# A routed expert block whose 186 slots per expert are laid over the partitions as 128 + 58 instead of 96 + 90

## The chip, the cores and the metric

One NeuronCore of one Trainium2 chip runs the whole program in one launch. The metric is the device time in microseconds (us); the kernel before was run three times. An execution with the hardware profiler switched on is timed as well, and all instruction times below come from that execution.

## The reference

The input is 32 images of 3 x 96 x 96. They are cut into 36 patches each, projected to 256 features, given a class token and a position table (37 tokens per image, N = 32 x 37 = 1184 tokens), put through an attention-like block with running sums, and then through a mixture of 8 experts. The part that matters here is the last one:

```
logits = xf @ w_router + b_router            # 1184 x 8
topv, topi = top_k(softmax(logits), 2)       # two experts per token
cap = int(1.25 * n / e)                      # 185 slots per expert
pos = cumsum(onehot)[...] - 1 ; keep = pos < cap
buf[expert, slot] = xf[token]                # gather
h   = gelu(buf @ w1 + b1) ; out = h @ w2 + b2   # 185 x 256 -> 1024 -> 256
y[token] += weight * out[expert, slot]       # scatter, weights normalised per token
```

All data is float32 and the result is 1184 rows of 256 features.

## The kernel before

Capacity 185 is rounded up to `SL = 186` slots. TensorE multiplies matrices that have the feature dimension on the partitions and the 186 slots along the free dimension, so the up projection (`up`, line 1170), the first expert's down projection (`down`, line 1180) and the split-precision down projection (`down_split`, lines 1193 and 1195) always work on 186 or 2 x 186 columns. Slots lie over partitions only where rows of tokens are moved. There they need two tiles, because 186 is more than 128 partitions. Lines 16 to 21 set how:

```
SLOT_TILES = 2
SL = CAP + CAP % 2
ST = 96
SIZES = [min(ST, SL - s * ST) for s in range(SLOT_TILES)]   # [96, 90]
```

The places where `ST` and `SIZES` act, in the order of the work:

- VectorE, `find_slots` (line 938), builds `at_p`, a bf16 one-hot of `ST` columns for each of 11 token tiles and 2 choices. It is made in two pieces. The first covers token tiles 0 to 2 (2 x 3 x `ST` elements per partition) and runs ahead of `take_in(0, 0, first=True)` (line 890), which makes the first expert's input. The second covers tiles 3 to 10 (2 x 8 x `ST` elements), and `id_marks` (line 948) and `marks_ready` follow it.
- TensorE, `look_up` (line 995): 22 matmuls with a weight load of `at_p` (111 or 74 partitions by `ST` columns, bf16) each. It runs twice, once for the token numbers of the slots (32 moving columns) and once for the gate weights (48 moving columns). The result lies on `ST` partitions. VectorE turns the first result into `src_row` and `dst_row` (lines 866 to 871).
- GpSimd (POOL), `gather` (line 460), starts for each expert from 1 to 7 one indirect DMA per slot tile, which brings `SIZES[s]` rows of 1 KB each from `xrows` into `rows_in`. Expert 0 is not gathered; its input comes from matmuls with a one-hot matrix (`pick`).
- TensorE, `turn_in` (line 1158): four transposes per gathered expert, whose identity matrix, the moving operand, has `SIZES[s]` columns.
- TensorE, `turn_out` (line 1203): four transposes per expert, with weight loads of `SIZES[s]` columns and 128 moving columns.
- ScalarE, `weigh` (line 620), scales the rows in two instructions, of `SIZES[s]` partitions each.
- POOL, `add_out` (line 475), starts two indirect DMAs per expert, which add `SIZES[s]` rows of 1 KB to `out_rows`. Before the first of each expert it waits until both of the expert before have landed.
- The last expert goes another way: `down_rows` (lines 1216 to 1220) makes rows directly, with 24 matmuls per slot tile whose weight loads have `SIZES[s]` columns and which move 256 columns each. VectorE (line 984) scales a tile as soon as it is done, and each tile's scatter waits for that tile alone.
- Two plain DMAs on the SP queue have this shape as well: the zeros behind the output rows (line 389) and the last expert's bias rows (line 409).

The order of the work is written out by hand for each engine. From expert 1 to expert 6 a loop runs on every engine; on TensorE its body is `up` of pair 0, `turn_out` of the expert before, `up` of pairs 1 to 3, `down_split` with `turn_in` of the next expert in its middle. SP loads the next `w1` and `w2` (1 MB each) during the loop.

Of the kernel before, what the change touches and what calls it, by code (L numbers as in the profile page):

```python
# [16 lines left out]
SLOT_TILES = 2  # L17
PAIRS = KF // 2
SL = CAP + CAP % 2
ST = 96  # L20
SIZES = [min(ST, SL - s * ST) for s in range(SLOT_TILES)]
TB = 3
TT = TB * T
# [37 lines left out]
def constants():  # L61
# [13 lines left out]

    c[:, C_TRASH] = N + p + ST * (np.arange(SC)[None, :] % SLOT_TILES)
    c[:, C_EPS] = EPS
# [14 lines left out]
def vit_block(nc, first, patches, const, vectors, attn, w1, w2, b2_rows, xrows, out):  # L92
# [6 lines left out]
    with ExitStack() as ctx:  # L99
        def sb(name, shape, dt=f32):  # L100
            return ctx.enter_context(nc.sbuf_tensor(name, shape, dt))
# [9 lines left out]
        ids = cst[0:TT, C_IDS]  # L111
        trash = cst[0:ST, C_TRASH]
        eps_col = cst[:, C_EPS]
# [41 lines left out]
        onehot = sb("onehot", [TT, NT, SL])  # L155
        rows_in = [sb(f"rows_in{q}", [ST, SLOT_TILES, D]) for q in range(2)]
        def held(i, k):
            return first_t[:, :, :].rearrange("p k d -> p (k d)")[:, i * SL:(i + k) * SL].rearrange("p (k s) -> p k s", k=k)
# [3 lines left out]
        out_t, out_low = held(KF + 2 * KD, KD), held(KF + 3 * KD, KD)  # L162
        out_s = [sb(f"out_s{q}", [ST, SLOT_TILES, D]) for q in range(2)]

# [13 lines left out]
        neg_prefix = sb("neg_prefix", [TT, TT], bf16)  # L178
        zeros = sb("zeros", [ST, D])
        bn = sb("bn", [TT, 2 * NT, 6])  # L180
# [1119 lines left out]
```

How the kernel before makes its waits and increments, by code:

```python
        def drained(eng, kind, n):  # L310
            step = last_read(kind, n)
            if step in DVE_READS:
                eng.wait_ge(dve_drained, DVE_READS.index(step) + 1)
            else:
                eng.wait_ge(act_drained, ACT_READS.index(step) + 1)
# [14 lines left out]
        def filled(eng, kind, n):  # L331
            eng.wait_ge(psum_filled, PLACE[kind, n] + 1)
            return slots_at(n) if kind == "slots" else slot(kind, n)
# [26 lines left out]
        @block.sync  # L361
# [11 lines left out]
                    sp.dma_start(cst[:, :], const).then_inc(const_in, 16)  # L373
            def load_w1(e, q):
                sp.dma_start(w1_s[q], w1[e].rearrange("(k p) f -> p k f", p=128)).then_inc(w1_in[q], 16)
            def load_w2(e, q):
                sp.dma_start(w2_s[q], w2[e].rearrange("(k p) d -> p k d", p=128)).then_inc(w2_in[q], 16)
            for e in range(2):
                if e == 1:
                    sp.wait_ge(psum_filled, PLACE["proj", len(GROUPS) - 1] + 1)
                load_w1(e, e)
                load_w2(e, e)
            sp.wait_ge(pool_set, 2)
            for s, size in enumerate(SIZES):
                sp.dma_start(out[N + s * ST:N + s * ST + size], zeros[0:size, :]).then_inc(out_stored, 16)
# [13 lines left out]
                store_rows(out, h2, t0, n, out_stored)  # L404
            sp.wait_ge(gathered[1], 16 * SLOT_TILES)
            for n in range(len(GROUPS)):
# [3 lines left out]
                for q in range(2):  # L411
                    e = 2 * i + q + 2
                    sp.wait_ge(up_done, (e - 1) * PAIRS)
                    load_w1(e, q)
```

## Time and profile before

| | us |
|---|---|
| median of 3 runs (167.69 to 168.73) | 168.11 |
| profiled execution, its own time | 169.34 |
| span of that execution, first to last instruction | 167.5 |
| TensorE matmul busy | 157.5 (94%) |
| VectorE busy | 111.4 (67%) |
| ScalarE busy | 77.4 (46%) |
| POOL busy | 51.7 (31%) |

Busy times are unions of intervals; matmuls are pipelined, so their durations overlap and the distance between two starts is what one of them costs. "PEld" is the weight load of a matmul, on the same engine, "POOLq" and "PEq" are sequencers, "SPq" is the queue on which SyncE starts DMAs. L995 is line 995. The profiled execution's own time is 1.2 us above the median of the runs; the working below uses its durations as differences.

### The profile page before, as it was taken

Reading aid. Unit: us, or ns where it says so; the run is one execution under the profiler, and the core shown is the slowest. Engines: PE = TensorE matmul, PEld = TensorE weight load, DVE = VectorE, ACT = ScalarE, POOL = GpSimd, SP = SyncE. Lnnn points to the kernel's source line nnn. Section 1 sums busy time; section 2 is a strip of 40 time slices with the busy share of each in tenths; the row PEclk is TensorE's granted clock in tenths of the full one; section 3 lists DMA queues with packets and bytes.
Section 4 is the critical chain, followed back from the end, with each engine's and each line's share of the span. In section 5 each row is a group of like instructions: output and inputs, shape, how many; then the busy total and the mean of one; then the engine's idle time right before and its main releaser. Section 6 shows DMA issues by size and latency. Waiting matters only on the chain.

```text
span 167.5 us, 3069 instructions
## 1 busy us (share of the span) xinstructions
PE 157.5 (94%) x1041; PEld 148.2 (88%) x1041; DVE 111.4 (67%) x361; ACT 77.4 (46%) x186; POOL 51.7 (31%) x51
## 2 busy tenths in 40 slices
PE   7999999999999789989989999999999999999960
PEld 7679999986886689979989999999999999999950
DVE  0077673688588998396948876948669486694620
ACT  4306543526452309343705737657365583655300
POOL 2006213043021000000721735627266272703351
PEclk9999999999999955899999999999999999999995
DMA  5999930096014410620158789887888868820422
GB/s 164 429 411 420 386 125 0 9 337 206 0 29 134 122 45 4 195 59 4 45 175 308 144 287 268 248 266 137 287 253 255 263 145 276 245 22 6 46 25 22
DMA packets 17264, 28.48 MB, mean 170 GB/s; under 512 B 1289, under 2 KB 13875, under 8 KB 17125
## 3 DMA queue, kind: packets, MB, share of 16 engines
q1 hardware_dynamic: 14789, 25.48, 45.2%
q0 software_dynamic: 2464, 2.86, 10.0%
q8 instruction: 6, 0.10, 0.2%
q14 instruction: 5, 0.04, 0.1%
HBM read 24.20 MB, written 4.14 MB: 169 GB/s over the span
## 4 chain that ended last, share of the span: by engine, by line
PE 77%; DVE 14%; issue 2%; POOL 2%; DMA 1%; POOLq 1%; DVEq 0%
PE ps L1170 21%; PE ps L1193 11%; PE ps L1091 7%; PE ps L1076 6%; PE ps L1030 6%; PE ps L1195 5%; PE ps L1011 4%; DVE prod L777 2%; DVE z_s L775 2%; PE ps L1203 2%; PE ps L1042 2%; DVE onehot L752 2%; PE ps L1180 2%; PE ps L1158 2%; DMA rows_in<-xrows,src_row 1%
## 5 line engine op out<-in xcount | busy, mean ns | idle before, releaser
L475 POOL DMA_INDIRECT out_rows<-out_s,dst_row x16 | 23.7, 1483 | 40.4 <-ACT out_s L620 34.1
L596 ACT ACTIVATE first_t<-ps,b_cur 128x186 f32<-128x186 f32 x64 | 23.1, 412 | 25.5 <-PE ps L1170 25.5
L1193 PE MATMUL ps<-hid_hl,split 128*128 128x372 f32 x96 | 29.0, 369 | 0.0
L460 POOL DMA_INDIRECT rows_in<-xrows,src_row x14 | 15.7, 1124 | 33.2 <-DVE src_row L868 29.2
L1195 PE MATMUL ps<-hid_hl,split 128*128 128x186 f32 x96 | 23.9, 249 | 0.0
L1170 PE MATMUL ps<-first_t,w_even 128*128 128x186 f32 x128 | 21.8, 322 | 0.7 <-DVE first_t L890 0.7
L1170 PE MATMUL ps<-first_t,patch_t 128*128 128x186 f32 x128 | 21.6, 321 | 0.0
L899 DVE CAST hid_hl<-first_t 128x372 fp32r<-128x372 f32 x28 | 10.7, 383 | 16.1 <-ACT first_t L596 16.1
L1170 PEld LDWEIGHTS ps<-first_t,w_even 128*128 128x128 f32 x128 | 20.1, 190 | 1.0 <-issue 1.0
L1170 PEld LDWEIGHTS ps<-first_t,patch_t 128*128 128x128 f32 x128 | 20.1, 190 | 0.0
L1195 PEld LDWEIGHTS ps<-hid_hl,split 128*128 128x128 f32 x96 | 18.3, 191 | 0.0
L1193 PEld LDWEIGHTS ps<-hid_hl,split 128*128 128x128 f32 x96 | 18.0, 188 | 0.0
L498 ACT ACTIVATE split<-patch_t 128x512 fp32r<-128x512 f32 (+1 forms) x28 | 13.9, 559 | 7.8 <-DMA patch_t<-patches 5.0
L901 DVE TENSOR_TENSOR hid_hl<-first_t,hid_hl 128x372 fp32r<-128x372 f32 x28 | 15.3, 547 | 1.0
L514 ACT ACTIVATE xn<-ps,nmr,rstd 111x256 f32<-111x256 f32 (+1 forms) x22 | 10.7, 557 | 4.0 <-DVE nmr L682 4.0
L1076 PE MATMUL ps<-split 128*128 128x324 f32 x72 | 11.1, 312 | 0.0
L1076 PEld LDWEIGHTS ps<-split 128*128 128x128 f32 x72 | 10.7, 188 | 0.0
L661 DVE BATCH_NORM_STATS2 bn<-ps 111x6 f32<-111x256 f32 (+1 forms) x22 | 8.0, 417 | 3.8 <-PE ps L1106 2.7
L1011 PE MATMUL ps<-onehot,xn 111*128 111x186 f32 (+1 forms) x44 | 10.4, 409 | 0.1
L907 DVE TENSOR_TENSOR split<-patch_t,split 128x512 fp32r<-128x512 f32 x16 | 10.2, 685 | 0.0
L505 ACT ACTIVATE std<-mv,cst 111x3 f32<-111x3 f32 (+2 forms) x10 | 2.7, 294 | 16.0 <-DVE mv L664 16.0
L1011 PEld LDWEIGHTS ps<-onehot,xn 111*128 111x128 f32 (+1 forms) x44 | 9.8, 255 | 0.3 <-DVE by_expert L759 0.2
(165 smaller groups left out, 272.9 us busy)
## 6 DMA issues: line engine op xcount, KB each, us to landing
w_even<-w SPq DMA_DIRECT2D x8, 1024.0 KB, 5.3
patch_t<-w SPq DMA_DIRECT2D x8, 1024.0 KB, 5.3
patch_t<-patches SPq DMA_DIRECT2D x2, 972.0 KB, 11.2
att<-attn SPq DMA_DIRECT2D x1, 1280.0 KB, 8.4
first_t<-first SPq DMA_DIRECT2D x1, 870.0 KB, 6.0
xrows<-xn SPq DMA_DIRECT2D x3, 288.0 KB, 2.4
out_rows<-h SPq DMA_DIRECT2D x3, 288.0 KB
first_t<-first SPq DMA_DIRECT2D x1, 580.0 KB, 4.2
```

The source lines that it names most:

```text
L460: pool.indirect_dma_start(out=rows_in[q][0:SIZES[s], s, :], out_offset=None, in_=xrows[:, :], in_offset=bass.IndirectOffsetOnAxis(ap=src_r ...
L475: pool.indirect_dma_start(out=out[:, :], out_offset=bass.IndirectOffsetOnAxis(ap=dst_row[0:SIZES[s], c:c + 1], axis=0), in_=out_s[q][0:SIZ ...
L498: return act.activation(dst, src, ACT.Copy)
L514: ins = act.activation(xn[0:r, t], p[0:r, i * D:(i + 1) * D], ACT.Identity, bias=nmr[0:r, base + t:base + t + 1], scale=rstd[0:r, base + t ...
L596: ins = act.activation(hid[:, f, :], bank(pair)[:, (f % 2) * SL:(f % 2 + 1) * SL], ACT.Gelu, bias=b1_cur[q][:, f:f + 1])
L901: dve.tensor_tensor(hid_hl[:, f, 1], hid[:, f], hid_hl[:, f, 0], ALU.subtract).then_inc(hid_split, 1)
L1011: ins = pe.matmul(pick_slot[:, k, :], xn[0:r, t, k * 128:(k + 1) * 128], onehot[0:r, t, :], start=t == 0, stop=t == NT - 1)
L1076: ins = pe.matmul(p[:, d * 512:d * 512 + nb * NP2], w[:, k, d * 128:(d + 1) * 128], x[:, k, :], start=k + m == 0, stop=k == KP - 1 and m == 2)
L1091: ins = pe.matmul(p[:, d * 512:d * 512 + nb * NP2], tok_wt[:, k, d * 128:(d + 1) * 128], src[:, k, :], start=k == 0, stop=k == KP - 1)
L1170: ins = pe.matmul(bank(pair)[:, (f % 2) * SL:(f % 2 + 1) * SL], w1_s[q][:, k, f * 128:(f + 1) * 128], buf_t[q][:, k, :], start=k == 0, sto ...
L1193: pe.matmul(dst[:, 0:2 * SL], w2_h[q][:, f, cols], hid_hl[:, f].rearrange("p a s -> p (a s)"), start=f == 0, stop=False)
L1195: ins = pe.matmul(dst[:, 0:SL], w2_l[q][:, f, cols], hid_hl[:, f, 0], start=False, stop=f == KF - 1)
```

## The change

One constant. The slots of an expert stand as 128 + 58 over the partitions instead of 96 + 90; `SIZES` becomes `[128, 58]`.

```diff
 SLOT_TILES = 2
 PAIRS = KF // 2
 SL = CAP + CAP % 2
-ST = 96
+ST = 128
 SIZES = [min(ST, SL - s * ST) for s in range(SLOT_TILES)]
```

What it touches: `at_p` becomes 11 x 2 x 128 wide, `look_up` loads 128 weight columns, `slot_id`, `src_row`, `dst_row` and `coef` stand on 128 partitions, each gather and each scatter is 128 rows and 58 rows, the transposes are 128 and 58, and the two row products of the last expert make 128 and 58 rows.

## Rows read from the trace of the kernel before

**Rows 1.** The page, part 4: chain of work that ended last, by engine

```profile
PE 77%; DVE 14%; issue 2%; POOL 2%; DMA 1%; POOLq 1%; DVEq 0%
```

**Rows 2.** The same chain from 73 to 90 us: start, duration, what

```profile
77.49 1.18 PE ps L995 x22
...
80.19 1.15 POOL rows_in L460
...
81.64 2.36 DMA rows_in<-xrows,src_row
```

**Rows 3.** Waits from 73 to 90 us: who waited for whom, us, times, longest

```profile
PEld ps L1158 <- DMA rows_in<-xrows,src_row: 0.8, 1, 0.8
PE ps L1170 <- DVE first_t L890: 0.7, 1, 0.7
PEld ps L995 <- DVE id_marks L948: 0.4, 1, 0.4
```

**Rows 4.** Groups by line and form: shapes, count, busy us, mean ns, idle before

```profile
L938 DVE TENSOR_TENSOR at_p<-cst,slot_p 111x1536 bf16<-111x1536 f32 x1 | 1.8, 1752 | 0.0
L938 DVE TENSOR_TENSOR at_p<-cst,slot_p 111x576 bf16<-111x576 f32 x1 | 0.8, 750 | 0.0
L995 PE MATMUL ps<-w_marks,at_p 111*96 111x48 bf16 x20 | 1.0, 202 | 0.0
L995 PEld LDWEIGHTS ps<-w_marks,at_p 111*96 111x96 bf16 x20 | 1.0, 125 | 0.0
L1146 PEld LDWEIGHTS ps<-chosen,ones 111*111 111x111 bf16 x5 | 0.3, 133 | 0.0
L1158 PE MATMUL ps<-cst,rows_in 90*128 90x90 f32 x14 | 2.9, 242 | 0.0
L1203 PE MATMUL ps<-cst,first_t 128*90 128x128 f32 x14 | 2.7, 273 | 0.0
```

**Rows 5.** Timeline of TensorE around bf16 loads: start, first start to last end

```profile
69.38 0.34 PEld L1146 LDWEIGHTS ps<-chosen,ones 111*111 111x111 bf16 x5
77.49 1.06 PEld L995 LDWEIGHTS ps<-id_marks,at_p 111*96 111x96 bf16 x22 [0.37 <-DVE id_marks L948]
84.69 0.23 PE L995 MATMUL ps<-w_marks,at_p 111*96 111x48 bf16 x2
```

**Rows 6.** Timeline of TensorE in the expert loop: both kinds of transposes

```profile
95.43 0.49 PE L1158 MATMUL ps<-cst,rows_in 96*128 96x96 f32 x4
99.89 0.60 PE L1203 MATMUL ps<-cst,first_t 128*96 128x128 f32 x4
```

**Rows 7.** Timeline of TensorE and POOL in the last expert

```profile
158.67 0.28 PE L1220 MATMUL ps<-split,hid_hl 128*96 128x256 f32 x1
160.00 1.45 POOL L475 DMA_INDIRECT out_rows<-out_s,dst_row  x1 [3.10 <-DVE out_s L984]
161.49 0.28 PE L1220 MATMUL ps<-split,hid_hl 128*90 128x256 f32 x1
162.59 1.47 POOL L475 DMA_INDIRECT out_rows<-out_s,dst_row  x1 [1.14 <-DVE out_s L984]
```

**Rows 8.** DMA, 83.2 to 84.2 us, the 90-row gather: queue, packets, MB, share

```profile
q0 software_dynamic: 48, 0.09, 31.6%
```

**Rows 9.** DMA of the 96-row scatter (161.9 to 163.2), then the 90-row (164.5 to 167.5)

```profile
DMA packets 112, 0.10 MB, mean 76 GB/s; under 512 B 16, under 2 KB 112, under 8 KB 112
...
DMA packets 112, 0.09 MB, mean 31 GB/s; under 512 B 22, under 2 KB 112, under 8 KB 112
q0 software_dynamic: 112, 0.09, 30.9%
```

**Rows 10.** Windows: stretch, length, busy of PE, PEld, DVE, ACT, POOL, PEclk, DMA

```profile
56.00:58.00 2.00, 1.43 (x14) 1.43 (x15) 1.86 (x16) 0.00 (x0) 0.00 (x0) 1.00 0.63 169
58.00:60.00 2.00, 1.65 (x14) 1.59 (x13) 1.93 (x14) 0.00 (x0) 0.00 (x0) 0.50 0.57 172
74.00:76.00 2.00, 1.36 (x9) 1.39 (x10) 2.00 (x5) 0.27 (x2) 0.00 (x0) 1.00 0.00 0
```

## The prediction

> **What bounds the kernel now.** I read the chain of waits first. It lies on TensorE for 77% of the span, on VectorE for 14% and on GpSimd and DMA for a few per cent [rows 1]. So TensorE sets the time, except in short stretches, and an edit is worth what it does to TensorE's spacing or to one of those stretches. The change touches three places of the second half: the set-up of the slots (73 to 90 us), the loop over experts, and the last expert's tail. The part of the chain from 73 to 90 us shows that the set-up is serial: behind at_p and the marks on VectorE come the look-up on TensorE, the first gather's start on POOL and the landing of its second DMA [rows 2]. The waits of that stretch say where TensorE stood still: 0.7 us for the first expert's input, which VectorE makes behind the first piece of at_p, 0.4 us for the marks behind the second piece, 0.8 us for the first gather [rows 3]. Afterwards the chain stays on TensorE to its last product: the list of waits has no later one of it on a gather or a scatter. The end is one VectorE instruction, one scatter and its landing [rows 7].
>
> **at_p gets wider.** The two pieces of 576 and 1536 elements took 750 and 1752 ns [rows 4]. The slope is 1002/960 = 1.044 ns per element. They become 768 and 2048 elements: +192 is +0.20 us, +512 is +0.53 us. The first delays take_in(0) and with it TensorE, which was waiting for just that [rows 3]; the second delays the marks, for which TensorE also waits, and nothing else covers it. Both lie on the path: +0.73 us.
>
> **Look-ups, 2 x 22 matmuls.** The weight load grows from 96 to 128 bf16 columns. From the timeline, the 22 loads take 1.06 us from first start to last end with 0.125 us for one, so (1.06 - 0.125)/21 = 44.5 ns apart; the 5 loads of 111 columns are (0.34 - 0.133)/4 = 52 ns apart [rows 4, 5]. The moving side has 32 and 48 columns, and with a load ready in time two such matmuls stood (0.23 - 0.202) = 28 ns apart [rows 4, 5]. So the load sets the spacing and costs 0.5 ns per column: 128 columns give 60.5 ns, +16 ns x 44 = +0.70 us. Bounds: 28 ns apart (44 x -16.5 = -0.73 us) if the load stops limiting, and 83 ns, the distance at which 128-column f32 loads are known to fit (transposes, below), +1.7 us. I take +0.70, since the two nearest widths lie on that line. The first look-up delays src_row and the gather, the second delays TensorE itself; both are on the path.
>
> Against this stands a rule. The Trainium skill, page "TensorE: Matmul & The Clock Gate", section "Weight-path perf modes — Fast Weight Load (FWL) and DoubleRow", says that loads of exactly 128 non-fp32 weight columns take a faster path by themselves. No bf16 load of 128 columns is in this trace. By the rule the 44 loads would get cheaper rather than dearer; that is rival 1.
>
> **Gathers.** POOL's issue time does not follow the rows: the last 96-row scatter took 1.45 us and the 90-row one 1.47, and that is kept [rows 7]. Only the first gather is on the path, and there its second DMA, since that is issued 1.45 us after the first and lands last [rows 2]. That DMA kept the 16 engines 31.6% busy over 1 us, 5.06 engine-us; over 15 engines with data that is 0.34 us for 6 rows each [rows 8]. With 58 rows over 16 engines it is 4 rows each: -0.10 us (bounds 0 and -0.2). The 128-row DMA before it gets 8 rows per engine instead of 6, ends some 0.1 us later, and has over a microsecond until the second's data. The later gathers are issued a whole expert ahead, and TensorE waits for none of them; uncovered, each would move by the same 0.1 us.
>
> **Transposes.** turn_in: four starts within 0.49 us, (0.49 - 0.242)/3 = 83 ns apart at 96 and 90 moving columns, with a load of 128 columns for each. turn_out: (0.60 - 0.273)/3 = 109 ns apart at 128 moving columns [rows 4, 6]. So a 128-column move costs 109 ns; one of 58 lies between 58/128 x 109 = 49 ns (move-bound) and 83 ns (bound by its 128-column load, which is known to fit in 83). Per expert 2 x 109 + 2 x (49 to 83) against 332 ns: -16 to +52 ns; I take 61 ns for the short one, the spacing a 128-column load gets above, +8 ns. Seven experts: +0.06, rounded to +0.1 us (-0.1 to +0.4). turn_out keeps its 128 moving columns at 109 ns, which hides a load of 128 (83) as well as 96: 0, or up to 16 ns for each expert's first load, which I leave in the range.
>
> **Last expert.** The row products with 90-column loads stand (161.49 - 158.67)/24 = 117.5 ns apart [rows 7]. The 256 moving columns set that. 128 and 58 change nothing: a 128-column load fits in 83 ns. ScalarE's and VectorE's instructions keep their free sizes; the partitions of a tile do not appear in their durations (the groups of L984 and L620 at 96 and 90 partitions agree).
>
> **Tail.** The last scatter's DMA kept 16 engines 30.9% busy over 3 us: 14.8 engine-us over 96 slots of 6 on each engine, 0.155 us a row, 0.93 us an engine [rows 9]. 58 rows are 4 per engine: -0.31 us (bounds 0 and -0.4), right at the end of the span. The 128-row scatter ahead of it gets 0.31 us longer but its data move from 162 us on and the last one's only after 164.5 [rows 9].
>
> **The plain DMAs.** The zeros are stored in the first half and asked for by the first scatter; the bias rows (128 KB for 96) are loaded ahead of the loop and used in the last expert. The loop and the set-up hide them; uncovered, 32 KB more at the gather's rate (0.34 us for 90 KB) is 0.1 us.
>
> **Sum.** 0.73 + 0.70 - 0.10 + 0.10 - 0.31 = +1.12 us. On the profiled execution that is 169.34 + 1.12 = 170.5; that execution stands 1.23 us above the median of the runs, 168.11, to which I apply the same difference: 169.2 us, +0.7%. A measurement of this kernel tells no less than 1% (1.7 us) from no change, so this is "no change", on the slow side.
>
> **Rival 1: the wide loads are quick.** If a 128-column bf16 load no longer limits, the moving side does: 28 ns apart, 44 x -16.5 = -0.73 us. Sum 0.73 - 0.73 - 0.10 + 0.10 - 0.31 = -0.31 us, 167.8 us. For it: these 44 are the only loads that change from another width to 128 in bf16. Against: the line through 96 and 111 columns. This is the case of the skill's rule named above.
>
> **Rival 2, slower: 58 rows go over two engines.** If a DMA's rows are dealt only to as many engines as divide their number, 96 goes to 16, 90 to 15, 128 to 16, but 58 = 2 x 29 to two, 29 rows each. It decides from the size at which the divisor falls below the engines needed to stay hidden, here at two places. The first gather: 29/6 x 0.34 = 1.64 us instead of 0.34, +1.30 us. The last scatter: 29 x 0.155 = 4.5 us instead of 0.93, +3.6 us. In between POOL's idle time before scatters hides it. Total 0.73 + 0.70 + 0.10 + 1.30 + 3.6 = +6.4 us, 174.5 us (about 172.5 if accumulating rows pipeline better in a long run). What speaks against it: the 96-row scatter left 112 packets of which 16 are small, that is 96 rows and one semaphore write per engine; the 90-row one also left 112, of which 22 small, so 90 rows were filled up to 96 with 6 tiny packets [rows 9]. Filling up to a multiple of 16 is dealing by 16, and 58 would be filled to 64. It is not conclusive, since 15 x 6 rows and one engine of 6 fillers is also what divisor dealing with equal rings leaves.
>
> The Trainium skill, page "DMA: Bandwidth & Descriptors", section "Why a DMA increments its semaphore by 16 and not by 1", states the divisor rule, and also an exception measured on software-generated direct copies, rounded up over 16 engines. The packet counts here sit with the exception.
>
> **Rival 3: the clock falls.** TensorE's granted clock went to 0.50 (1.2 GHz) at 58 us after 2 us with 1.43 us busy in thin products; in 74 to 76 us with 1.36 us busy it stayed at 1.00 (2.4 GHz) [rows 10]. The change adds 0.2 and 0.53 us of standing and thinner look-ups there. A fall like the one at 58 us, over about 10 us of work, costs up to 5 us: 174. Against it: dense products lie between the gaps.
>
> **How the numbers follow.** Main case 0.53 (169.2; its own bounds 168.2 to 170.2), rival 1 0.27 (167.8), rival 2 0.09, rival 3 0.04, something unforeseen 0.07 on both sides. The predicted time is the main case's. The range 167.4 to 170.4 takes in the main case with its bounds and rival 1 with some noise of the runs (0.5 us each way), and leaves out rivals 2 and 3 and most of the unforeseen, 0.18. Slower by over 1% means above 169.8: rivals 2 and 3, a fifth of the main case (0.11), half the unforeseen: 0.27. Faster means below 166.4: 0.04. Within 1%: 0.69.
>
> **What would show it.** at_p at 0.95 and 2.29 us; TensorE's waits before the first expert and before the look-up longer by 0.2 and 0.5 us; the 22 look-up loads 60 ns apart (right) or about 30 (rival 1); in the last scatter 80 packets, 64 + 16, with 22 under 512 B, and its landing about 0.3 us sooner after issue (right), or a landing 3 us and more later with a low DMA share (rival 2); turn_in's four transposes in about 0.50 us; the clock at 1.00 from 68 us to the last product (else rival 3). Wrong would be a new wait of TensorE inside the loop, or a look-up or DMA whose cost does not follow these rows.

## The result and the profile after

The changed kernel takes 183.33 us (median of 4 runs, 182.31 to 184.81) against 168.38 us for the kernel before on the same chip. The ratio is 1.089, 95% interval 1.084 to 1.094: 15 us slower. Forecast was 169.2 us (167.4 to 170.4). The profiled execution has a span of 181.5 us, 14.0 more than before. Here and below the ratios leave out the few executions of the chip's slower state (the longest were one of 864.71 us of the version with 80 moved rows and one of 260.51 us of the kernel before).

The page of the changed kernel: span, DMA packets, the software queue, and the chain that ended last.

```profile
span 181.5 us, 3069 instructions
...
DMA packets 21155, 28.55 MB, mean 157 GB/s; under 512 B 5246, under 2 KB 17878, under 8 KB 21016
...
q0 software_dynamic: 6336, 2.90, 10.7%
...
PE 49%; DMA 20%; DVE 14%; POOL 5%; issue 4%; ACT 2%; POOLq 1%; ACTq 0%; DVEq 0%
DMA out_rows<-out_s,dst_row 18%; PE ps L1170 7%; PE ps L1091 6%; PE ps L1076 6%; PE ps L1030 6%; PE ps L1193 5%; POOL out_rows L475 4%; PE ps L1011 4%; DMA rows_in<-xrows,src_row 2%; PE ps L1180 2%; PE ps L1195 2%; PE ps L1158 2%; ACT out_s L620 2%; DVE prod L777 2%; DVE z_s L775 2%
```

Before, 77% of the chain lay on TensorE and the DMAs had 1% [rows 1]. Now the scatters alone hold 18%. The software queue, which carries the indirect DMAs, moves nearly the same bytes (2.90 MB, before 2.86) with 6336 packets where the kernel before had 2464 on its page.

Last two scatters of the changed kernel: DMA from 173.5 to 175.4 us (128 rows), then from 175.9 to 179.9 us (58 rows).

```profile
DMA packets 144, 0.13 MB, mean 69 GB/s; under 512 B 16, under 2 KB 144, under 8 KB 144
q0 software_dynamic: 144, 0.13, 63.5%
...
DMA packets 480, 0.06 MB, mean 16 GB/s; under 512 B 422, under 2 KB 480, under 8 KB 480
q0 software_dynamic: 480, 0.06, 17.3%
```

The 128-row scatter is 128 rows and 16 semaphore writes. The 58-row one is 58 rows, 16 semaphore writes and 406 fillers, tiny packets without a row: 480 = 16 x (29 + 1). So two engines carry 29 rows each, and the other fourteen carry 29 fillers. In the 90-row scatter of before [rows 9] the six fillers were the sixteenth engine's share beside 15 x 6.

Waits of the changed kernel over the whole span: who waited for whom, us in total, times, longest.

```profile
POOL out_rows L475 <- issue: 8.4, 9, 5.9
...
ACT out_s L620 <- POOLq L470: 4.4, 4, 1.9
...
PEld ps L1158 <- DMA rows_in<-xrows,src_row: 2.7, 1, 2.7
```

The wait for the first gather was 0.8 us [rows 3] and is 2.7 (counted at the weight loads; 2.4 at the matmuls). ScalarE's scaling of an expert's rows now waits four times until POOL has seen both scatters of the expert before land; the kernel before has no such wait. POOL stood 5.9 us before the last expert's first scatter. The row puts that down to "issue", but there the code waits for the same landing.

The scatters on the chain of the changed kernel, three of them: start, time until landed.

```profile
108.72 7.72 DMA out_rows<-out_s,dst_row
119.65 8.85 DMA out_rows<-out_s,dst_row
163.38 6.88 DMA out_rows<-out_s,dst_row
```

The last of these lands at 170.3 us, and POOL's next scatter starts at 171.44.

Timeline of POOL in the changed kernel, last two experts: start, duration, idle before.

```profile
161.50 1.58 POOL L475 DMA_INDIRECT out_rows<-out_s,dst_row  x1 [5.80 <-ACT out_s L620]
163.38 2.12 POOL L475 DMA_INDIRECT out_rows<-out_s,dst_row  x1 [0.30 <-issue]
171.44 1.57 POOL L475 DMA_INDIRECT out_rows<-out_s,dst_row  x1 [5.93 <-issue]
173.32 2.09 POOL L475 DMA_INDIRECT out_rows<-out_s,dst_row  x1 [0.30 <-issue]
```

The last scatter starts at 173.32 instead of 162.59 [rows 7]; the span ends 8.2 us after that start, not 4.9. POOL's own time for the 58-row scatter is 2.1 us against 1.47 for 90 rows.

When the rows of the second tile were ready for that last scatter, before and then changed (VectorE's scaling).

```profile
161.81 0.48 DVE L984 SCALAR_TENSOR_TENSOR out_s<-ps,coef,z_s 90x256 f32<-90x256 f32 x1 [2.25 <-PE ps L1220]
```

```profile
169.75 0.48 DVE L984 SCALAR_TENSOR_TENSOR out_s<-ps,coef,z_s 58x256 f32<-58x256 f32 x1 [2.23 <-PE ps L1220]
```

Before, the scatter started 0.3 us after its rows were ready. In the changed kernel they were ready at 170.23 us and the scatter started 3.1 us later, so 2.8 us of POOL's 5.9 reach the end of the span.

Timeline of the set-up in the changed kernel: VectorE's at_p, TensorE's look-up loads and the first transposes.

```profile
72.99 0.95 DVE L938 TENSOR_TENSOR at_p<-cst,slot_p 111x768 bf16<-111x768 f32 x1
...
74.26 2.28 DVE L938 TENSOR_TENSOR at_p<-cst,slot_p 111x2048 bf16<-111x2048 f32 x1
...
77.72 0.61 PEld L995 LDWEIGHTS ps<-id_marks,at_p 111*128 111x128 bf16 x22 [0.90 <-DVE id_marks L948]
...
85.96 0.99 PE L1158 MATMUL ps<-cst,rows_in 128*128 128x128 f32 x4 [2.37 <-DMA rows_in<-xrows,src_row]
```

The four transposes of the same expert in the kernel before:

```profile
84.30 0.55 PE L1158 MATMUL ps<-cst,rows_in 96*128 96x96 f32 x4 [0.50 <-DMA rows_in<-xrows,src_row]
```

at_p is as forecast. The 22 loads are (0.61 - 0.096)/21 = 24.5 ns apart (a load is 96 ns in the groups), not 60: the look-ups got cheaper. The four transposes take 0.99 us where they took 0.55. In the loop it is 0.93 against 0.49 [rows 6].

Windows of the changed kernel: stretch, length, busy of PE, PEld, DVE, ACT, POOL, PEclk, DMA share, GB/s.

```profile
84.00:86.00 2.00, 0.04 (x1) 0.04 (x1) 0.00 (x0) 0.00 (x0) 1.25 (x2) 1.00 0.28 93
...
88.00:92.00 4.00, 4.00 (x17) 4.00 (x16) 1.40 (x9) 0.00 (x0) 0.00 (x0) 0.57 0.68 240
```

Two of these microseconds in the kernel before:

```profile
88.00:90.00 2.00, 2.00 (x16) 1.97 (x15) 1.53 (x3) 0.26 (x1) 0.00 (x0) 1.00 0.87 316
```

TensorE stood for 2.4 us waiting for the gather, and behind it its granted clock fell to 1.2 GHz for most of four microseconds; 0.57 of the full clock over 4 us is 4 x 0.43 = 1.7 us of dense work lost. Before, this stretch ran at 2.4 GHz.

### The profile page after: what moved, and what is told of

Its sections match the earlier page's. It is cut to its first block, busy times and chain, and to the rows that moved or that the text cites. A ratio compares the mean times of both kernels' runs of the same rounds, so it can differ in the third digit from the quotient of the medians.

```text
span 181.5 us, 3069 instructions
## 1 busy us (share of the span) xinstructions
PE 160.9 (89%) x1041; PEld 148.4 (82%) x1041; DVE 111.9 (62%) x361; ACT 77.9 (43%) x186; POOL 61.3 (34%) x51
## 3 DMA queue, kind: packets, MB, share of 16 engines
q0 software_dynamic: 6336, 2.90, 10.7%
## 4 chain that ended last, share of the span: by engine, by line
PE 49%; DMA 20%; DVE 14%; POOL 5%; issue 4%; ACT 2%; POOLq 1%; ACTq 0%; DVEq 0%
DMA out_rows<-out_s,dst_row 18%; PE ps L1170 7%; PE ps L1091 6%; PE ps L1076 6%; PE ps L1030 6%; PE ps L1193 5%; POOL out_rows L475 4%; PE ps L1011 4%; DMA rows_in<-xrows,src_row 2%; PE ps L1180 2%; PE ps L1195 2%; PE ps L1158 2%; ACT out_s L620 2%; DVE prod L777 2%; DVE z_s L775 2%
## 5 line engine op out<-in xcount | busy, mean ns | idle before, releaser
L475 POOL DMA_INDIRECT out_rows<-out_s,dst_row x16 | 30.2, 1889 | 42.4 <-ACT out_s L620 34.0
L460 POOL DMA_INDIRECT rows_in<-xrows,src_row x14 | 18.8, 1346 | 33.3 <-DVE src_row L868 29.3
```

Source lines behind the costliest of these rows:

```text
L460: pool.indirect_dma_start(out=rows_in[q][0:SIZES[s], s, :], out_offset=None, in_=xrows[:, :], in_offset=bass.IndirectOffsetOnAxis(ap=src_r ...
L475: pool.indirect_dma_start(out=out[:, :], out_offset=bass.IndirectOffsetOnAxis(ap=dst_row[0:SIZES[s], c:c + 1], axis=0), in_=out_s[q][0:SIZ ...
```

## Experiments

All ratios are to the kernel before on the same chip. Theory T was: (a) an indirect DMA goes to the largest number of engines, up to 16, that divides its row count, the others get as many fillers; (b) changing between matmuls over at most 64 and over more than 64 partitions keeps the next weight load from running ahead of the matmul in front of it.

**Another short second tile, with good divisors.**

```diff
-ST = 128
+ST = 126
```

> Tile sizes 126 + 60 instead of 128 + 58. Theory T: an indirect DMA is dealt to the largest number of engines up to 16 that divides its rows, so 126 goes to 14 and 60 to 15 engines (9 and 4 rows each), no long gather or scatter; the fillers nearly vanish. The transposes of turn_in still alternate between more and fewer than 64 rows and keep their 0.86 us (0.58 us more than before) per expert. Loads of 126 bf16 columns in the look-ups 59 ns apart, not 25. Time: 168.4 + 4.0 (transposes) + 0.7 (at_p) + 0.7 (look-ups) - 0.3 (tail) = 173.5 us. Theory U (an uneven split, or a DMA under 64 rows, is itself slow, whatever its divisors): 181 to 184 us, as with 128 + 58.

Measured 174.07 us, ratio 1.035 (1.030 to 1.039). From the page of this kernel:

```profile
q0 software_dynamic: 2592, 2.86, 10.1%
```

2592 is what theory T counts. The scatters make 8 x (16 x 9 + 16 + 16 x 4 + 16) = 1920 packets. The gathers, whose packets by these counts hold up to 4 rows, make 7 x (16 x 3 + 16 + 16 + 16) = 672. Its first look-up and its transposes in the timeline of TensorE:

```profile
77.89 1.44 PE L995 MATMUL ps<-id_marks,at_p 111*126 111x32 bf16 x22 [0.58 <-DVE id_marks L948]
...
96.89 0.93 PE L1158 MATMUL ps<-cst,rows_in 126*128 126x126 f32 x4
```

One constant moved by two gives back 9 us. An uneven split or a DMA under 64 rows is not slow by itself. The transposes are as dear as with 58, and the look-up takes 1.44 us, where 128 columns take 0.71 (a row of the kernel with 64 moved rows, below): of the widths run here only the full 128 columns are quick.

**A longer second tile, with a bad divisor.**

```diff
-ST = 128
+ST = 112
```

> Tile sizes 112 + 74. Theory T: 74 = 2 x 37 rows go to two engines, 37 each with 14 x 37 fillers, so the gather's and scatter's second DMA is longer than with 58 rows; each expert's scatter lands some 2 us later than with 58 and the chain of scatters sets the time of every expert: 195 to 200 us. Both tiles have more than 64 rows, so turn_in's transposes are 83 ns apart as before (0.29 us until the next product). Theory U (DMAs under 64 rows are slow): 74 rows are well, about 169 us.

Measured 189.97 us, ratio 1.126 (1.118 to 1.134). Page, then waits of this kernel:

```profile
q0 software_dynamic: 7456, 2.91, 11.0%
```

```profile
ACT out_s L620 <- POOLq L470: 10.0, 6, 2.4
PEld ps L1158 <- DMA rows_in<-xrows,src_row: 4.9, 2, 3.2
```

Theory U, the rival in the expectation, is out: this kernel has no DMA under 64 rows, its 126 + 60 sister was quick, and 112 and 74 have 16 and 2 as their divisors. The size was forecast too high (195 to 200), since the loop waits 10.0 us for scatters where I had taken the chain of scatters to bound every expert. The second wait for a gather lies inside the loop. Its transposes, from the timeline of TensorE, are not disturbed by 74 rows:

```profile
98.82 0.50 PE L1158 MATMUL ps<-cst,rows_in 112*128 112x112 f32 x4
99.11 0.42 PE L1193 MATMUL ps<-hid_hl,split 128*128 128x372 f32 x1
```

**Rows filled up to 64 in both DMAs of the short tile.**

```diff
+MOVED_IN = [128, 64]
+MOVED_OUT = [128, 64]
...
-                        out=rows_in[q][0:SIZES[s], s, :], out_offset=None, in_=xrows[:, :],
+                        out=rows_in[q][0:MOVED_IN[s], s, :], out_offset=None, in_=xrows[:, :],
...
-                        in_=out_s[q][0:SIZES[s], s, :], in_offset=None, compute_op=ALU.add,
+                        in_=out_s[q][0:MOVED_OUT[s], s, :], in_offset=None, compute_op=ALU.add,
```

(the index columns likewise; VectorE clears the spare rows once at the start, and the output has six more spare rows)

> 128 + 58 as in the changed kernel, but the second gather and scatter of each expert move 64 rows (six idle slots: row 0 is gathered, zeros are added to spare rows behind the output). 64 divides by 16: 4 rows on each engine. Theory T: all long DMAs vanish, with them the clock's fall at 88 us and the waits in the loop; what is left is turn_in, +4.0 us over seven experts, at_p +0.7, look-ups -0.9, tail -0.3: 168.4 + 3.5 = 171.9 us. Theory V (a good part of the 15 us is not the second DMA but something else in 128 + 58, for instance POOL's longer descriptor making for 128 rows): above 175 us.

Measured 172.77 us, ratio 1.025 (1.020 to 1.030): 10.6 us of the 15 belong to the two DMAs of 58 rows. Timeline of TensorE:

```profile
78.20 0.71 PE L999 MATMUL ps<-id_marks,at_p 111*128 111x32 bf16 x22 [0.62 <-DVE id_marks L952]
...
95.84 0.93 PE L1162 MATMUL ps<-cst,rows_in 128*128 128x128 f32 x4
96.70 0.44 PE L1197 MATMUL ps<-hid_hl,split 128*128 128x372 f32 x1
```

**One of the two at a time.** The same edit for the gather alone, and for the scatter alone.

> 128 + 58 with only the second gather at 64 rows; the second scatter stays at 58 rows on two engines. The gather's long wait goes (1.9 us) and with it the fall of the clock at 88 us (1.7 us); the chain of scatters and the long tail stay: 183.3 - 3.6 = 179.7 us. Rival (the clock falls for another reason than the gather's wait): the clock's 3.4 us at 0.50 stay, 181.4 us.

Measured 179.78 us, ratio 1.068 (1.061 to 1.075). The window behind the first gather:

```profile
88.00:92.00 4.00, 4.00 (x29) 3.98 (x28) 3.89 (x8) 2.19 (x7) 1.29 (x1) 1.00 0.88 289
```

> 128 + 58 with only the second scatter at 64 rows; the second gather stays at 58 rows on two engines. Tail and the waits for the scatters in the loop go, about 7.5 us; the wait for the first gather and the fall of the clock stay: 183.3 - 7.5 = 175.8 us. Rival (the loop's waits come from gathers too): over 177 us.

Measured 175.35 us, ratio 1.041 (1.035 to 1.047). The same window:

```profile
88.00:92.00 4.00, 4.00 (x19) 4.00 (x18) 1.47 (x8) 0.00 (x0) 0.00 (x0) 0.68 0.60 227
```

So the gather costs 183.33 - 179.78 = 3.6 us and the scatter 183.33 - 175.35 = 8.0; together 10.6, a little less than the sum. The clock stays at 2.4 GHz where the gather is short and falls where it is long, whatever the scatters do: the fall follows the wait. Of the scatter's 8.0 us, 2.8 are the late start of the last one and 3.3 its longer landing. About 2 us are left for the waits in the loop, although ScalarE's add up to 4.4, so they do not reach the end in full.

**Order of the transposes** (on the kernel with 64 moved rows).

```diff
-                for k in range(KD):
-                    for s, size in enumerate(SIZES):
+                for s, size in enumerate(SIZES):
+                    for k in range(KD):
                         ins = pe.transpose(bank(5)...
```

> As the kernel with 64 moved rows, and turn_in makes both transposes of the 128-row tile first and then both of the 58-row tile. If the cost lies in each change between a matmul with up to 64 rows and one with more (four changes per expert before, two now), turn_in shrinks from 0.86 to about 0.57 us, -2.0 us in all: 169.9 us. If every 58-row transpose is dear by itself, nothing changes: 171.9 us.

Measured 169.61 us, ratio 1.007 (1.004 to 1.011), 3.2 us less than the same kernel in the old order. Timeline of TensorE:

```profile
94.61 0.64 PE L1162 MATMUL ps<-cst,rows_in 128*128 128x128 f32 x4
95.19 0.44 PE L1197 MATMUL ps<-hid_hl,split 128*128 128x372 f32 x1
```

The next product starts 0.58 us after the first transpose, not 0.86: 7 x 0.28 = 2.0 us are explained by it as forecast. Of the other 1.2 us, the profiled executions show 0.8 ahead of any transpose: at_p starts at 72.63 us here and at 73.46 with 64 moved rows in the old order. Both kernels do the same up to there, so that part is no effect of the order (these starts lie between 71.55 and 73.55 us in the profiled executions of all versions). The same four instructions in another order are cheaper, so the cost is in the changes, not in a 58-row transpose. Against 0.33 us without a change (128 and 66 rows, below), four changes cost 0.53 us and two cost 0.25: 0.13 us for each.

Weight loads of the transposes in this version, then in the kernel before.

```profile
94.93 0.20 PEld L1162 LDWEIGHTS ps<-cst,rows_in 58*128 58x128 f32 x2 [0.17 <-issue]
```

```profile
95.34 0.39 PEld L1158 LDWEIGHTS ps<-cst,rows_in 96*128 96x128 f32 x4
```

Before, the four loads follow each other without a gap, and the first starts 0.09 us ahead of its transpose (95.43). Here the loads of 58 rows begin only after a gap of 0.17 us, at the change.

**More than 64 rows in the short tile's transposes**: the gather brings 80 rows and the transposes work on 80.

```diff
-MOVED_IN = [128, 64]
+MOVED_IN = [128, 80]
...
-                    for s, size in enumerate(SIZES):
+                    for s, size in enumerate(MOVED_IN):
```

> As the kernel with 64 moved rows, but the second gather brings 80 rows (5 on each of 16 engines) and the second tile's transposes work on 80 rows and columns, in the first order (128, 80, 128, 80). Theory T (the cost is the change between up to 64 and more than 64 rows): no such change is left, the transposes are 83 to 110 ns apart as before, -3.5 to -4 us against the kernel with 64 moved rows: 168.4 + 0.7 - 0.9 - 0.3 + 0.2 = 168.2 us. If order and not row count mattered: 172.5 us.

Measured 169.22 us, ratio 1.004 (1.000 to 1.007). With this kernel as base, two versions of one run each place the border; only the transposes' row count differs.

```diff
-                    for s, size in enumerate(MOVED_IN):
+                    for s, size in enumerate((128, 64)):      # and (128, 66)
```

> As the kernel with an 80-row gather, but the second tile's transposes read 64 rows. If the border lies at 64 rows included, the next product starts 0.86 us after the first transpose, as with 58. If it lies lower, 0.35 us.

> The same with 66 rows: over 64, so the four transposes and the start of the next product take about 0.35 us, as with 80 rows.

They gave 172.8 us with 64 rows and 167.94 us with 66, one run each. That is 4.9 us apart, where the transposes explain 7 x 0.54 = 3.8; at_p starts 1.5 us earlier in the second (71.55 against 73.08), ahead of anything that differs. Timelines of TensorE with 80, with 64 and with 66 rows:

```profile
93.78 0.53 PE L1162 MATMUL ps<-cst,rows_in 128*128 128x128 f32 x4
94.12 0.44 PE L1197 MATMUL ps<-hid_hl,split 128*128 128x372 f32 x1
```

```profile
95.68 0.94 PE L1162 MATMUL ps<-cst,rows_in 128*128 128x128 f32 x4
96.55 0.43 PE L1197 MATMUL ps<-hid_hl,split 128*128 128x372 f32 x1
```

```profile
93.45 0.51 PE L1162 MATMUL ps<-cst,rows_in 128*128 128x128 f32 x4
93.78 0.44 PE L1197 MATMUL ps<-hid_hl,split 128*128 128x372 f32 x1
```

0.34, 0.87 and 0.33 us to the next product: 64 rows belong to the dear side, 66 to the cheap one.

**Two controls of the divisor rule** on either side of the kernel before.

```diff
-ST = 128
+ST = 120        # and ST = 93
```

> Tile sizes 120 + 66, one constant against the kernels before and after. Theory T: 120 rows go to 15 engines (8 each), 66 to 11 (6 each), both tiles have more than 64 rows, so neither long DMAs nor dear transposes; loads of 120 bf16 columns 56 to 57 ns apart. 168.6 + 0.5 (at_p) + 0.5 (look-ups) = 169.6 us. Theory U (uneven splits are slow by themselves): 175 us and more.

Measured 170.11 us, ratio 1.010 (1.006 to 1.015). Its page has the packets that 15 and 11 engines make, 8 x (16 x 8 + 16 + 16 x 6 + 16) + 7 x 96 = 2720:

```profile
q0 software_dynamic: 2720, 2.86, 9.9%
```

> Tile sizes 93 + 93, as even a split as there is and hardly another work than 96 + 90. Theory T: 93 = 3 x 31, so every gather and scatter goes to 3 engines, 31 rows each, with 13 x 31 fillers. The first gather lands 2 us later, the clock falls behind it, the scatters take 3 us longer each and set the loop's pace: about 180 us (178 to 184). Theory U (uneven or short DMAs are slow): 168.4 us.

Measured 189.98 us, ratio 1.124 (1.112 to 1.136). The page and the waits of this kernel:

```profile
q0 software_dynamic: 10208, 2.93, 11.3%
```

```profile
ACT out_s L620 <- POOLq L470: 13.8, 6, 2.8
PEld ps L1158 <- DMA rows_in<-xrows,src_row: 3.6, 2, 3.3
```

The even split that differs from 96 + 90 by three rows is as slow as 112 + 74 (189.98 and 189.97 us), because both its tiles are 3 x 31. 10208 = 8 x 2 x (16 x 31 + 16) + 7 x 2 x (16 x 8 + 16). I had forecast 180: that both scatters of an expert are long, and the loop waits 13.8 us for them rather than 4.4, was in no term of mine.

**The wide load without the wide tiles**: the kernel before, with at_p stored 128 columns wide. VectorE still writes 96, POOL clears the other 32 once at the start.

```diff
+LOADED = 128
...
-        at_p = sb("at_p", [TT, NT, 2, ST], bf16)
+        at_p = sb("at_p", [TT, NT, 2, LOADED], bf16)
...
+            pool.memset(at_p[:, :, :, ST:LOADED], 0.0).then_inc(pool_set, 1)
...
-                return dve.tensor_tensor(at_p[:, a:b], grid(iota_slot[:, 0:ST], b - a, 2, ST),
+                return dve.tensor_tensor(at_p[:, a:b, :, 0:ST], grid(iota_slot[:, 0:ST], b - a, 2, ST),
...
-                        look_up(id_marks, bank(ID_BANK)[0:ST, 0:2 * SC]).then_inc(ids_looked, 1)
+                        look_up(id_marks, bank(ID_BANK)[0:LOADED, 0:2 * SC]).then_inc(ids_looked, 1)
```

(the second look-up likewise)

> The kernel before (96 + 90) in everything but the look-ups' weight load: at_p lies 128 columns wide, of which VectorE still writes 96 and POOL sets 32 to zero at the start, and the look-ups load 128. The 44 loads go from 45 to 25 ns apart: -0.88 us with nothing added, as both look-ups are on the path: 167.5 us. If a part is only moved into the waits behind it, -0.4 us: 168.0.

Measured 167.91 us against 168.78, ratio 0.995 (0.992 to 0.998). Timeline of its look-up loads:

```profile
76.90 0.62 PEld L997 LDWEIGHTS ps<-id_marks,at_p 111*128 111x128 bf16 x22 [0.37 <-DVE id_marks L950]
```

0.62 us where it was 1.06 [rows 5], twice: 0.88 us. The medians differ by 0.87 us (the interval allows 0.3 to 1.4), and from the start of at_p to the end the profiled executions take 93.2 us against 94.0. This is the one version with more than one run that beats both kernels.

## Why the prediction was wrong

- **What bounds the kernel.** Right for before; the forecast that nothing would take TensorE's place was wrong. In the changed kernel the scatters do in part: they hold 18% of the chain, and TensorE's share falls from 77% to 49%.
- **at_p, +0.73 us.** Right: 0.951 and 2.282 us, both on the path.
- **Look-ups, +0.70 us.** Wrong in sign. The line through 96 and 111 columns does not reach 128, because 128 goes another way. Rival 1 had it (28 ns forecast, 24.5 measured), the step was sized by the wrong rows. In all 44 loads -0.88 us. The Trainium skill, page "TensorE: Matmul & The Clock Gate", section "Weight-path perf modes — Fast Weight Load (FWL) and DoubleRow", has the faster path for exactly 128 columns; the trace agrees, 24.5 ns apart at 128 and 57 to 58 at 126.
- **Gathers and tail, -0.10 and -0.31 us: the step that failed.** It put both DMAs down as gains, because it read six fillers in the 90-row scatter as "filling up to a multiple of 16" and so dealt 58 rows four to an engine. They cost 3.6 and 8.0 us. The same text named the other reading, equal rings behind divisor dealing, and gave it 0.09. The runs show that one: 406 fillers and 29 rows on each of two engines, and packet counts that fit to the packet in five kernels (128 + 58, 126 + 60, 112 + 74, 120 + 66, 93 + 93). Packets cannot tell the readings apart where ceil(rows/16) is rows/15; 90 is such a number. The Trainium skill, page "DMA: Bandwidth & Descriptors", section "Why a DMA increments its semaphore by 16 and not by 1", gives the divisor rule and an exception for some direct copies. I let the exception stand for indirect DMAs, for which it does not claim anything. Here the indirect ones all follow the divisor rule.
- **Rival 2's price, 174.5 us.** Its mechanism is what happened and its size was too small. The gather's wait grew by 1.9 us (1.3 forecast), and it pulled the clock down for another 1.7 us. That is rival 3's mechanism at another place, set off by rival 2; I had priced the two as if independent. The last scatter ends 3.3 us later after its start (3.6 forecast). But "POOL's idle time before scatters hides it" was wrong: the next expert's scatter waits for both of the last one, ScalarE waits for that (4.4 us in four times), and at the end, where `down_rows` makes the last tiles early, POOL stood 5.9 us, 2.8 of which reach the end of the span.
- **Transposes, +0.1 us.** Wrong, 3.6 us (ratios 1.025 against 1.004). The spacing of 83 ns for a 128-column load was read from pairs in which all transposes have over 64 rows. Next to a 58-row one the load no longer runs ahead (the gap of 0.17 us above), and each change costs 0.13 us. The Trainium skill, page "TensorEngine Tiling (Array Packing)", section "Key Properties", says that changing the tiling mode drains TensorE, and its section "When to Use Tiling" puts row tiling at a contraction of 64 or less. I did not weigh it, since nothing in the code asks for tiling. The trace agrees with the border (64 dear, 66 cheap); that the 58-row transposes run in such a mode is shown by no run. The column side shows nothing of the kind: `turn_out` with loads of 58 columns keeps 109 ns, 0.60 us for four as before [rows 6], and the row products of the last expert run as before.
- **How the 15 us divide:** 10.6 in the two DMAs (183.33 to 172.77), 3.6 in the transposes (172.77 to 169.22), and 0.6 that the kernel with 80 moved rows still has over before (its ratio of 1.004 times 168; the interval allows 0.05 to 1.2). The 3.6 agree with the timelines, 7 x (0.86 - 0.34) = 3.6. at_p and the look-ups make 0.73 - 0.88 = -0.15 of the 0.6. The remaining 0.8 was not isolated by a run; the version with 80 moved rows has waits of TensorE that neither the kernel before nor the one with 64 moved rows has, three ahead of `turn_out` for VectorE:

```profile
PEld ps L1207 <- DVE first_t L916: 1.5, 3, 0.7
```

## What to carry to other kernels

Before a tile size is changed, factor the row count of every indirect DMA that it sets: in every version here the largest divisor up to 16 is the number of engines that carry rows. Spare rows are cheap next to a bad divisor (58 filled up to 64 gave back 10.6 us). Keep the contraction of neighbouring matmuls on one side of 64 partitions, or group them. And widen a bf16 weight load to 128 columns if it sets the pace, with columns that nobody reads (0.9 us for 44 loads).

## What the hardware showed that was not expected

- An indirect scatter gives every engine without rows as many tiny packets as the others have rows (406 for 58 rows). POOL's time to issue a scatter goes with the packets and not with the rows: 1.45 us for 80 packets (64 rows), 1.6 for 144 (128 rows), 2.1 to 2.2 for 480 (58 rows), 2.3 to 2.7 for 608 (74 rows).
- In the loop, beside 1 MB weight loads, an accumulating scatter of 29 rows on each of two engines took 7.7 to 8.9 us until it had landed, by the chain of waits, and 6.9 in the last expert but one.
- bf16 weight loads stood 44.5 ns apart at 96 columns, 52 at 111, 51 at 112, about 55 at 120, 57 to 58 at 126, and 24.5 at 128.
- Four transposes and the start of the next product: 0.33 us with 128 and 66 rows alternating, 0.87 with 128 and 64; 0.58 with 128, 128, 58, 58.
